# Decays spread by broadcast loads through DRAM instead of PE transposes, in an audio tower with a Mamba-2 block and a mixture of experts

## What is computed

```
scale = where(wnorm < 1, 1, 1 / wnorm)                 # norm of a window of 9 frames
h  = relu(tanh(conv9(x) * scale) + bias)               # 32 x 248 x 128
z, xBC, dt = split(layernorm(h) @ in_proj_w)           # 256, 256+64+64, 4
xs, B, C   = split(silu(causal_conv4(xBC) + conv_b))
dt    = softplus(dt + dt_bias);   decay = exp(dt * -exp(A_log))       # 4 heads
state = decay_t * state + (dt_t * x_t) B_t^T;   y_t = state C_t + D_skip * x_t
h  = h + (rms_norm(y * silu(z)) * norm_w) @ out_proj_w
h  = h + MoE(layernorm(h))       # 16 experts, top 2, a shared expert, a last FFN
```

## Time and profile before

| | |
|---|---|
| median of 3 runs | 1026.23 us (1022.69 to 1026.74) |
| the profiled execution, its span | 1024.98 us, 1023.1 us |
| mean granted PE clock | 0.945 |
| busy share of the span: PE, DVE, ACT, POOL | 89%, 71%, 49%, 57% |
| pipeline (22 steps) | 0 to about 585 us |
| expert blocks, last FFN | about 585 to 887, 887 to 1023 us |
| a step of the pipeline, mean over 15 | 30.1 us |

### The profile page before, as it was taken

How to read it: one execution, slowest core, us unless ns; L and a number is a source line. 1 busy time by engine, 2 the same in 40 slices (tenths; PEclk the granted TensorE clock), 3 DMA queues, 4 the chain that set the end, 5 groups by cost and what they waited for, 6 DMA issues and landing times.

```text
span 1023.1 us, 22359 instructions
## 1 busy us (share of the span) xinstructions
PE 905.9 (89%) x6324; PEld 790.4 (77%) x6325; DVE 724.6 (71%) x2092; ACT 502.3 (49%) x1259; POOL 587.5 (57%) x649
## 2 busy tenths in 40 slices
PE   4697999999999999999874369999999998669998
PEld 3576877877877787887654269999999998558887
DVE  5357799888889989888874335555555554599993
ACT  3333555554555555555322125555555554555653
POOL 5435455777778777777646454444444444365551
PEclk9989999999999999999966679999999999879999
DMA  7400000110100110000095112232221221224332
GB/s 180 90 11 11 1 11 12 31 31 22 30 17 27 32 31 27 16 19 16 18 275 158 40 44 68 78 85 67 65 67 55 58 64 54 56 81 114 97 101 51
DMA packets 72057, 59.12 MB, mean 58 GB/s; under 512 B 19169, under 2 KB 61468, under 8 KB 71985
## 3 DMA queue, kind: packets, MB, share of 16 engines
q1 hardware_dynamic: 63440, 41.88, 15.9%
q0 software_dynamic: 8544, 16.34, 4.8%
HBM read 35.62 MB, written 23.81 MB: 58 GB/s over the span
## 4 chain that ended last, share of the span: by engine, by line
PE 48%; DVE 24%; issue 15%; POOL 8%; another core or an unknown queue 1%; ACT 1%; DMA 1%; SPq 0%; DVEq 0%; POOLq 0%; ACTq 0%
PE psum L967 13%; PE psum L952 13%; DVE arena L1504 4%; DVE arena L1852 4%; PE psum L650 3%; POOL x_slots L1362 3%; PE psum L651 3%; PE psum L652 3%; PE psum L785 2%; PE psum L802 2%; DVE h_all L1552 2%; DVE arena L1857 2%; PE psum L961 2%; POOL arena L1338 2%; DVE arena L1512 2%
## 5 line engine op out<-in xcount | busy, mean ns | idle before, releaser
L1189 ACT ACTIVATE arena<-psum,arena 128x128 f32<-128x128 f32 x556 | 159.0, 369 | 155.9 <-PE psum L952 131.9
L1395 POOL DMA_INDIRECT y_tokens<-arena x139 | 136.8, 984 | 161.0 <-DVE arena L1802 117.1
L952 PE MATMUL psum<-arena 128*128 128x128 f32 x1112 | 154.5, 283 | 27.2 <-DVE arena L1795 15.7
L952 PEld LDWEIGHTS psum<-arena 128*128 128x128 f32 x1112 | 139.9, 198 | 29.1 <-DVE arena L1789 15.3
L967 PE MATMUL psum<-arena 128*128 x1112 | 156.4, 284 | 0.4 <-issue 0.4
L1362 POOL DMA_INDIRECT x_slots<-arena,idx x128 | 128.0, 1000 | 34.6 <-issue 34.3
L967 PEld LDWEIGHTS psum<-arena 128*128 128x128 f32 x1112 | 137.6, 194 | 7.4 <-issue 0.6
L1789 DVE COPY arena<-arena 128x644 f32 x139 | 75.4, 542 | 72.1 <-issue 65.6
L1795 DVE TENSOR_SCALAR arena<-psum,lng,lnb 128x128 f32<-128x128 f32 x139 | 56.9, 409 | 52.5 <-PE psum L961 40.8
L1504 DVE TENSOR_TENSOR_SCAN arena<-psum,arena 124x496 f32<-124x496 f32 x64 | 72.5, 1175 | 11.9 <-PE psum L785 7.8
L1332 POOL TENSOR_TENSOR arena<-arena 128x496 f32<-128x496 f32 x32 | 40.0, 1251 | 34.6 <-DVE arena L1532 34.6
(11 more groups left out here) (283 smaller groups left out, 2215.8 us busy)
## 6 DMA issues: line engine op xcount, KB each, us to landing
arena<-x_slots SPq DMA_DIRECT2D x139, 64.5 KB
arena<-y_tokens SPq DMA_DIRECT2D x16, 448.0 KB
arena<-in_x SPq DMA_DIRECT2D x16, 256.0 KB, 3.2
out_tokens<-arena SPq DMA_DIRECT2D x16, 224.0 KB
y_tokens<-arena POOLq DMA_INDIRECT x139
x_slots<-zero_src SPq DMA_DIRECT2D x33, 64.5 KB, 4.2
moe_all<-in_x SPq DMA_DIRECT2D x4, 512.0 KB, 5.8
x_slots<-arena,idx POOLq DMA_INDIRECT x128
```

The source lines that it names most:

```text
L952: last = nc.tensor.matmul(psum[:, 2 + b.q % 2, k * 128:(k + 1) * 128], w1_blk[b.q % 4][:, k * 128:(k + 1) * 128], hT[b.q % 2], start=True, ...
L1189: last = nc.scalar.activation(EHT[t.q % 2][:, k * 128:(k + 1) * 128], psum[:, 2 + t.q % 2, k * 128:(k + 1) * 128], ACT.Silu, bias=w1_blk[t ...
L1395: nc.gpsimd.indirect_dma_start(out=y_tokens, out_offset=bass.IndirectOffsetOnAxis(ap=xb[t.q][:, F:F + 1].bitcast(i32), axis=0), in_=YO[t.q ...
```

## The change

The spreading moves from PE to the DMA engines. For unit b, in its own step: POOL makes the 16 columns of decays without the mask (two operations). PE transposes them at once, 124x16 to 16x124, into bank 1 (`dec_rows`). ACT copies the 16 rows twice to SBUF (`dec_copy`), once as they are with a zero in the first column (set before), once whole. DVE turns the second copy into running products along a chunk (`cum_decays`). SP stores eight rows of the first and four of the second for each n (`decays_out`, four stores) in a new DRAM tensor of 12 rows of 124 numbers for each n, waits for the four, and loads each n's 1488 numbers back on 124 partitions, every partition the same (`decays_in`, two loads of 738,048 bytes, into `DB[0]` and `DB[1]`). The scan then runs in place over eight rows of 124 at once (`scans`). The off-diagonal block, which had been a part of the long scan, is now the product of the last column of the first chunk's cumulated decays and a running product of the second chunk's, in `decayed_scores`: one 992-column operation and four of 124x124.

```diff
+                def decays_out(b):
+                    sp.wait_ge(S.cum_ready, b + 1)
+                    for n in range(2):
+                        later(sp, db_here[n], 16 * (b - 1))
+                    for n in range(2):
+                        sp.dma_start(dec_rows_of[b % 2, n, 0:8, :], dec_st[b % 2][8 * n:8 * n + 8, 0, :])\
+                            .then_inc(S.dec_stored, 16)
+                        sp.dma_start(dec_rows_of[b % 2, n, 8:12, :], dec_st[b % 2][8 * n + 4:8 * n + 8, 1, :])\
+                            .then_inc(S.dec_stored, 16)
+
+                def decays_in(b):
+                    sp.wait_ge(S.dec_stored, 64 * (b + 1))
+                    for n in range(2):
+                        later(sp, S.m_ready, 2 * (b - 1) + n + 1)
+                        sp.dma_start(DB[n].rearrange("p r t -> p (r t)"),
+                                     rows(dec_rows_of[b % 2, n].rearrange("r t -> (r t)"), CH)
+                                     .rearrange("p o t -> p (o t)"))\
+                            .then_inc(db_here[n], 16)
...
+                def scans(c, n):
+                    dve.wait_ge(db_here[n], 16 * (c + 1))
+                    o = DB[n][:, 0:8, :].rearrange("p r t -> p (r t)")
+                    V.tensor_tensor_scan(o, o, diag8.rearrange("p r t -> p (r t)"), 0.0, ALU.mult, ALU.add)\
+                        .then_inc(S.scan_done, 1)
...
+                    if c is not None: decayed_scores(c, 0)
                     if t == COUNT_AT + 1: full_blocks()
+                    if b is not None: dt_rest(b)
                     if b is not None: bc_taps(b)
-                    if b is not None: dt_rest(b)
-                    if c is not None: skip_add(c, 0); long_scans(c, 1); short_scans(c, 1); decayed_scores(c, 1)
+                    if c is not None: scans(c, 1); skip_add(c, 0); decayed_scores(c, 1)
                     if a is not None: stats(a)
...
                     if d is not None: logits(d)
+                    if b is not None: cum_decays(b)
...
+                    if c is not None: mean_squares(c)
+                    if b is not None: scans(b, 0)
+                    if a is not None: dt_first(a)
+                    if c is not None: residual(c)
+                    if at(t + 1, 0) is not None: x_rest(t + 1)
                     if c is not None: new_stats(c)
...
-                    if v is not None and v < UNITS - 5: scatter(v, (2, 3))
+                    if v is not None and v < UNITS - 5: scatter(v, (2,))
+                    if b is not None: decay_of(b)
                     if a is not None: add_bias(a)
                     if c is not None: gate(c, 0)
-                    if b is not None: decay_of(b)
+                    if v is not None and v < UNITS - 5: scatter(v, (3,))
...
+                    if a is not None: exp_of(a)
+                    if c is not None: rs8_of(c)
                     if early: scatter(u, (1,))
-                    if c is not None: rs8_of(c)
```

More of the change, by code:

```diff
@@ L269, in audio_tower @@
         pos[0] = 0
-        diag2 = take(CH, 2, L)
         w_out = take(128, 2, F)
@@ L318, in audio_tower @@
         dA = nab
-        ee2 = take(CH, 16)
+        pos[0] += 16
         free_at_gate = pos[0]
         Z, XT, BT, CT = [None] * 2, [None] * 2, [None] * 2, [None] * 2
+        dec_st = [None] * 2
         for q in (1, 0):
@@ L872, in shared_down @@
                         pe.wait_ge(S.table_ready, 1)
+                    if b is not None:
+                        pe.wait_ge(S.dect_copied, b + 1)
                     for j in range(4):
@@ L916, in _ @@
                         pe.wait_ge(consts_ready, 1)
-                    if c is not None: decays(c, 0); scores(c, 0)
                     if b is not None: dt_projection(b, t); bc_projection(b)
+                    if c is not None: scores(c, 0)
                     if a is not None: x_transposes(a)
@@ L921, in _ @@
                     if a is not None: conv(a, b)
-                    if d is not None: hh_transposes(d, a, t)
                     if c is not None: mix(c, 0)
@@ L925, in _ @@
                     for n in parts_at(t): windows(n)
-                    if c is not None: scores(c, 1); decays(c, 1)
+                    if c is not None: scores(c, 1)
+                    if d is not None: hh_transposes(d, a, t)
+                    if b is not None: projection(b, 1, None)
                     if m is not None: ranks(m, d)
@@ L932, in _ @@
                     if d is not None: logits(d)
-                    if b is not None: projection(b, 1, None); projection(b, 2, None); x_rows(b)
+                    if b is not None: dec_rows(b, a); projection(b, 2, None); x_rows(b)
                     if t == COUNT_AT + 1:
@@ L1166, in _ @@
                         high_part(2)
+                    if b is not None: silu(b, 0)
+                    if a is not None: convT_copy(a)
                     if d is not None: normed(d)
-                    if b is not None: silu(b, 0)
-                    if d is not None: stage(d)
-                    if a is not None: convT_copy(a)
+                    if a is not None: tanh(a)
+                    for n in parts_at(t): squares(n)
+                    if d is not None: hhT_copy(d); stage(d)
                     if b is not None: bc_silu(b)
-                    if d is not None: hhT_copy(d)
-                    if a is not None: tanh(a); relu(a)
-                    for n in parts_at(t): squares(n)
+                    if a is not None: relu(a)
+                    if b is not None: dec_copy(b)
                     if b is not None: silu(b, 1)
```

165 lines of the change are left out of this document (74 added, 91 removed).

## The result

| | before | changed |
|---|---|---|
| median | 1026.49 us (1022.69 to 1027.14) | 1094.93 us (1092.97 to 1096.86) |
| profiled execution, span | 1024.98, 1023.1 us | 1096.86, 1095.1 us |
| mean granted PE clock | 0.945 | 0.905 |
| ratio | 1 | 1.0666, interval 1.062 to 1.0712 |

The change costs 68 us by the medians, 72 in the two profiled executions; forecast were 1074 us, +49 against the profiled one, range 1015 to 1100. All of it arises in the pipeline: the first copy of the expert blocks starts at 657.88 us and before at 584.18, and what follows is as long as it was.

What follows compares the result with a forecast made beforehand. PE was taken as the bound before, with a DRAM round trip then closing a longer loop; start +6.7, t = 2 +0.7, steps 3 to 5 +6.9, 6 to 15 +36, 16 +2, tail -1: 1076, said as 1074 us, range 1015 to 1100.

Steps and rivals of the forecast that it cites:

- D: Time from cum_decays to the first load's landing: 13.5 us, of which stores and waits 3.7, load 2.0 fixed and 7.8 data.
- The path, steps with scatters: From scans(b, 0) to the next cum_decays in t = 6 to 15: 20.3 us; with the round trip 33.8 a step, +36.
- the four scatters: On POOL between row norms and decay_of, four scatters in a row: 5.06 us of the path.
- Steps 3 to 5: Steps without scatters: path 19.0 us and round trip 13.5, 32.5 a step against 30.2, +6.9 in all.
- Start: Unit 0's decays leave for DRAM at about 60 us, so conv of unit 2 begins at 76.7 and not 69.96: +6.7.
- t = 2: A smaller copy of the same wait in step 2, an estimate: +0.7 us.
- End: Step 16, the last with a projection: +2 us; from there on fewer PE transposes, the rest untouched: -1.
- PE idle: DVE idle about 6 us ahead of the scan of 992; PE busy 27.5 us a step, largest gap ahead of conv.
- the first rival: Loads over 16 engines, POOL chain sets 30.1 us a step, PE's clock falls behind the x_rows gap: 1031 us, chance 0.12.
- PE stays the bound: Rival: PE's work sets every step at 28.1 us, 13 steps of 2.1 less: 998 us, chance 0.05.

Runs made afterwards that it cites:

- e1: The changed kernel with each broadcast load issued as two, over partitions 0 to 111 and 112 to 123, on 16 engines; ratio to the kernel before 1.029.
- e7: e1 with scans(c, 1) ahead of dt_rest and bc_taps on DVE; one run, last residual at 587.3 us, steps with scatters 34.2 us.
- e3: e1 with POOL's order also changed, two and not four scatters between row norms and decay_of; ratio to the kernel before 0.969.
- e6: e1 with silu(b, 1) ahead of relu and dec_copy on ACT from step 5 on; ratio to the kernel before 1.016.
- e10: e3 with the first scan one place earlier on DVE, ahead of mean_squares; ratio to the kernel before 0.986.
- e11: e3 with the first scan back at the start of the next step; ratio to the kernel before 0.996.

## Why the prediction was right, and where it was short

The direction and the mechanism, a loop that a round trip over four DMA engines closes, held. The size did not hold as well: +49 us were forecast and +72 measured in the profiled execution, which lies 3 us inside the range. That it lies inside is in part luck, since the range was drawn from the stores' landing, the load's rate and the clock, and not from the terms that ran over. Point by point:

- **D.** Forecast 13.5 us, measured 12.97 in the step shown, and between 12.9 and 14.5 in all others but the last, which has 16.91. Inside it two terms were off against each other: the stores need 2.6 us from the first issue to the loads' issue and not 3.7 (they are issued in 0.3 us each, and landed in 1.6 and not 2.3), and the load 10.4 and not 9.8 (it moves 83 GB/s and not 94). The four engines, on which it rested, are shown by e1 and by the share of 0.25.
- **The path, steps with scatters.** Forecast 20.3, measured 21.65. All terms agree to about 0.1 us but one: the four scatters take 6.35 us (248.25 to 254.60) and not 5.06, since the scan of 992, with both inputs in SBUF, holds the fourth up (e7). That is the step that failed: I had taken 5.06 from a row where the scans beside it read PSUM. With it a step is 21.65 + 13.6 = 35.2 us as measured, against 33.8, and over ten steps that is 14 of the 22 us between +49 and +72.
- **Steps 3 to 5.** 32.5 forecast, 31.9 measured.
- **Start.** Forecast +6.7, measured +10.0 (conv of unit 2 at 79.98). The first cum_decays ended at 62.98 and not 60.1, since it waits 4.25 us for dec_copy, and its D was 13.85. With t = 2 the sizes were 3.3 and about 1 us short.
- **End.** Forecast +1 for step 16 and the tail, measured about +6 at the last residual. At the end of step 16 the last unit's scan waits 6.41 us for its load, and then PE stands 12.46 us ahead of mix (to 600.15) with nothing else to do. I had followed the loop only to the last projection. The loads of the expert weights run at the same time: the DMA share is 0.76 from the issue of this unit's loads at 578.80 to the scan at 593.15, and its D is 16.91 us. That they slow it is likely, and no run shows it.
- **PE idle.** I forecast a DVE wait of 6 us ahead of the scan and PE's largest gap ahead of conv. DVE waits 3.8 to 4.6 us in steps 3 to 5, but only 1.0 to 3.3 with scatters, because the rival's chain runs beside the loop, 1 to 2 us behind it: the gaps ahead of dec_rows and x_rows and half the clock were there, as the first rival had them. I had let them stand only where the loads are fast, and that was wrong; they are in the kernel either way. PE was busy 28.96 us of the step and not 27.5: from x_rows to row_sums it takes 12.4 us at the lower clock, and 9.9 before. e1 is that rival run: forecast 31.6 us a step (30.1 and 1.5 for the clock), measured 33.9. In one step of e1 (245.62 to 279.26, 33.6 us) the chain up to x_rows takes 21.7 us and not 20.3, for the scatter, and from there to row_sums 11.9, 2.0 for the clock and not 1.5.
- **PE stays the bound** (998 us): that is e3, once both chains are off the path, 28.4 us a step and a ratio of 0.969.
- **Slips in the prediction.** DVE's scans save 2.8 us by its own numbers and not 2.6, which nothing rests on. Its chances add up to 0.73 for slower and 0.06 for within 0.5%, where it says 0.70 and 0.09.

What stays open is at which gaps PE's clock falls: nearly equal ones were followed by 1.00 and by 0.50 in e6 (2.2 us) and in e10 (1.1 us), and e11 has gaps of 1.19 and 1.13 us with the clock at 1.00.

## What to carry to other kernels

Before moving work to DMA, divide: a load on 124 partitions ran on four engines of 16, and the same bytes in pieces of 112 and 12 on all of them. Put such a round trip where something else must happen anyway, follow the loop that it closes to the end of the pipeline, and look for the second chain close behind it; here either mend alone gave about 40 us (45 and 37) and both gave 102. And the scan with both inputs in SBUF was not free for GpSimd beside it, even where DVE itself had time.

## What was not expected of the hardware

- A scan of 124x992 whose inputs both lie in SBUF holds up what begins on GpSimd beside it, almost to its own end: 0.20 us became 2.12, 1.04 became 2.88, and an indirect DMA of 0.97 became 2.41 to 2.83. Scans and products with an input in PSUM held nothing.
- Small stores from SBUF to DRAM (2 to 4 KB, 4 or 8 rows) were issued in 0.3 us each and had landed 1.6 us after the last issue, against at least 2.7 for 64.5 KB.
- PE gaps of 2.21 and 2.26 us in two steps in a row (e6) were followed by a clock of 1.00 and of 0.50; of five gaps of 1.1 us (e10) four were followed by 0.50 and one by 1.00.
